# A mixture of experts and a LoRA layer in float32: one transfer of 256 KB per sample instead of four of 64 KB

## What is computed

```python
w = weight[adapter_ids]
y = jnp.einsum('bsi,boi->bso', x, w)
...
h = jnp.einsum('bsd,nrd->nbsr', y, lora_A)
coef = (SCALE * lora_weights)[:, None, None]
lora_out = jnp.einsum('nbsr,nor->bso', h, lora_B * coef)
out = x + jnp.einsum('bsd,od->bso', y, W) + bias + lora_out
```

## Time and profile before

| | |
|---|---|
| profiled execution | 1567.71 us |
| its span | 1566.0 us |
| median of three runs | 1570.32 us |
| PE busy | 1499.9 us (96%) |
| DVE, ACT, POOL busy | 780.1, 387.2, 470.0 us |
| stage one | products from 36 to 819 us |
| stage two | from 841 us to the end |
| moved by DMA | 257.74 MB, mean 165 GB/s |
| transfers of line 179 | 576 of 64 KB, median 3.0 us from issue to landing |

### The profile page before, as it was taken

One profiled execution on the slowest core, in us unless ns is written; L12 is line 12 of the kernel. 1 busy time (PEld: TensorE's weight loads), 2 busy tenths in 40 slices (PEclk: granted clock), 3 DMA queues, 4 the chain that ended last, 5 costly groups with the idle time before them and its releaser, 6 DMA issues.

```text
span 1566.0 us, 28094 instructions
## 1 busy us (share of the span) xinstructions
PE 1499.9 (96%) x6356; PEld 1198.7 (77%) x6357; DVE 780.1 (50%) x1202; ACT 387.2 (25%) x493; POOL 470.0 (30%) x656
## 2 busy tenths in 40 slices
PE   5849999999999999999996999999999999999998
PEld 3738888888888888888874888888888888888886
DVE  6556566766667666377764433333333333333331
ACT  4233333433433333244433110101010101010100
POOL 3433542334433433623332222222222222222221
PEclk9979999999999999999997999999999999999999
DMA  8987678858788776688867655555555555555553
GB/s 230 234 192 162 177 181 186 199 144 198 180 195 198 191 174 158 175 189 191 192 150 202 164 139 147 134 147 134 147 134 147 134 147 134 147 134 147 134 134 80
DMA packets 174549, 257.74 MB, mean 165 GB/s; under 512 B 22720, under 2 KB 130240, under 8 KB 174528
## 3 DMA queue, kind: packets, MB, share of 16 engines
q1 hardware_dynamic: 102944, 138.97, 38.4%
q10 hardware_dynamic: 52000, 76.57, 19.6%
q0 software_dynamic: 19584, 41.98, 9.7%
HBM read 181.93 MB, written 79.69 MB: 167 GB/s over the span
## 4 chain that ended last, share of the span: by engine, by line
PE 82%; DMA 6%; DVE 4%; issue 4%; ACT 2%; ACTq 1%; DVEq 1%; SPq 1%; POOLq 0%; POOL 0%
PE ps L632 27%; PE ps L633 27%; PE ps L634 27%; DMA w_raw<-in_L_cond_weight_dram 3%; DVE w_turn L437 1%; DVE w_lo L507 1%; DMA x_raw<-in_x_dram 1%; DVE x_turn L527 1%; ACT w_hi L333 1%; DMA w_raw<-weff 1%; DMA coef<-_L_ffn_lora_weights_dram 1%; SPq L192 1%; DMA weff<-stage 0%; ACT x_hi L341 0%; POOL x_raw L179 0%
## 5 line engine op out<-in xcount | busy, mean ns | idle before, releaser
L632 PE MATMUL ps<-w_hi,x_hi 128*128 x2096 | 832.8, 397 | 32.0 <-ACT stage L358 21.7
L633 PE MATMUL ps<-w_lo,x_hi 128*128 x2096 | 831.8, 397 | 0.0
L634 PE MATMUL ps<-w_hi,x_lo 128*128 x2096 | 831.5, 397 | 0.0
L632 PEld LDWEIGHTS ps<-w_hi,x_hi 128*128 128x128 f32 x2096 | 395.7, 189 | 130.0 <-issue 34.4
L634 PEld LDWEIGHTS ps<-w_hi,x_lo 128*128 128x128 f32 x2096 | 395.6, 189 | 96.1
L633 PEld LDWEIGHTS ps<-w_lo,x_hi 128*128 128x128 f32 x2096 | 395.8, 189 | 95.6
L179 POOL DMA_DIRECT2D x_raw<-in_x_dram x576 | 308.5, 540 | 508.1 <-DVE x_turn L527 364.2
L341 ACT ACTIVATE x_hi<-x_turn 128x512 fp32r<-128x512 f32 x272 | 160.2, 626 | 762.7 <-DVE x_turn L527 439.2
L313 POOL TENSOR_TENSOR stage<-stage,w_raw 128x1024 f32<-128x1024 f32 x64 | 154.0, 2407 | 566.1 <-DMA stage<-in_x_dram 566.1
L527 DVE STREAM_TRANSPOSE x_turn<-x_raw 128x256 f32<-128x256 f32 x544 | 193.7, 415 | 162.4 <-DMA x_raw<-in_x_dram 113.4
L534 DVE TENSOR_TENSOR x_lo<-x_turn,x_hi 128x512 fp32r<-128x512 f32 x272 | 177.4, 689 | 167.0 <-ACT x_hi L341 165.7
(11 more groups left out here) (75 smaller groups left out, 26.5 us busy)
## 6 DMA issues: line engine op xcount, KB each, us to landing
w_raw<-in_L_cond_weight_dram SPq DMA_DIRECT2D x256, 256.0 KB, 5.8
x_raw<-in_x_dram POOLq DMA_DIRECT2D x576, 64.0 KB, 3.0
y_scr<-stage ACTq DMA_DIRECT2D x144, 256.0 KB, 3.9
x_raw<-y_scr SPq DMA_DIRECT2D x128, 256.0 KB, 2.7
stage<-in_x_dram SPq DMA_DIRECT2D x128, 256.0 KB, 3.7
out_dram<-stage ACTq DMA_DIRECT2D x128, 256.0 KB, 2.9
weff<-stage ACTq DMA_DIRECT2D x8, 512.0 KB, 6.9
weff<-in_L_ffn_W_dram POOLq DMA_DIRECT2D x8, 512.0 KB, 14.9
```

Source lines behind the costliest of these rows:

```text
L632: mm(ps[b][:, cols], x_hi[b][:, t, :], hi, start=t == 0, stop=False)
L633: mm(ps[b][:, cols], x_hi[b][:, t, :], lo, start=False, stop=False)
L634: last = mm(ps[b][:, cols], x_lo[b][:, t, :], hi, start=False, stop=t == KT - 1)
```

## The change

`load_sample` issues one transfer of 256 KB onto all 128 partitions in place of the four. Its source is the sample, walked as segment q, then token pair j, then token m of the pair, in pieces of 256 numbers (1 KB), as before. DVE waits for one count of 16 on the sample's semaphore instead of four.

```diff
--- before.py
+++ after.py
@@ -174,10 +174,8 @@
             if not (isinstance(n, int) and n < 2):
 
                 eng.wait_ge(x_turned, 2 * n - 2)
-            rows = x[bass.ds(sample, 1)].rearrange("a (j m) n -> (a j) m n", m=2)
-            for q in range(QUADS):
-                eng.dma_start(x_raw[b][BLK * q:BLK * (q + 1), 2 * h:2 * h + 2, :],
-                              rows[:, :, q * SEG:(q + 1) * SEG]).then_inc(x_loaded[h][b], 16)
+            rows = x[bass.ds(sample, 1)].rearrange("a (j m) (q n) -> a q j m n", m=2, q=QUADS)
+            eng.dma_start(x_raw[b][:, 2 * h:2 * h + 2, :], rows).then_inc(x_loaded[h][b], 16)
 
         @block.sync
         def _(sp):
@@ -514,7 +512,7 @@
                         split_w(k, par, c - 1)
                 split_w(k, par, chunks[-1])
 
-            def prepare_x(n, b, raw, load, loaded=x_loaded, loads=QUADS):
+            def prepare_x(n, b, raw, load, loaded=x_loaded, loads=1):
 
                 for sems in loaded:
                     dve.wait_ge(sems[raw], load * (16 * loads) + 16 * loads)
```

## The result

The forecast was 1560.7 us, faster. The changed kernel is **slower**: its median is 1582.49 us (four runs, 1581.69 to 1583.7) beside 1570.17 us for the kernel before, 12.3 us more, a ratio of 1.0082 with a 95% interval of 1.0065 to 1.0098. The profiled execution took 1582.76 us with a span of 1581.1, against 1566.0 before. The interval leaves no doubt that it is slower, by under 1%. `load_sample`'s transfer is now line 178; all later lines stand two earlier than before.

A forecast was written before the change was run, and what follows sets the result against it. PE was 96% busy; GpSimd's issue of x bounded its second gap, expert 1's weights the first. Gains of 7.6 + 2.0 = 9.6 us took 1567.71 to 1558.1; 2.6 for the median made 1560.7 us, range 1556 to 1571.

The forecast's parts named there:

- Step 2: Landing of x: a new transfer lands 2.6 us after the end of its issue, bounds 2 and 6 us.
- The rival: Loads of x: 4 segments outermost in the source put each sample on 4 DMA engines; 1566.6 us, chance 0.30.
- the 2.0 are gone: First gap of PE: with each sample on 4 engines, tile 4 costs 2.4 us, cancelling the forecast's gain of 2.0.
- Step 4: First gap of PE, ending at 100.78 us: the first fold starts 2.4 us earlier, 2.0 us gained.
- tiles 0 to 2: nothing, 1 us either way: Start of the kernel, x landing among weights and stores: no gain counted, 1 us either way kept for the range.
- Step 5: Between 101 and 819 us: earlier x gains nothing; delayed weights could cost, with slot 66's margin at 2.2 us.
- Step 3: Gap of PE at unused slots 67 to 71: PE resumes at 833.0 instead of 840.65, 7.6 us gained.
- Step 1: GpSimd's issue of x: 1.50 us a sample instead of 2.36, bounds 0.86 and 2.16.
- The dearer issue: GpSimd's issue of x: a source order unlike the target's costs, say, 5 us a sample; 1588 us, chance 0.06.
- the same four engines every time: Stage one: x always on four engines, 2.5 us or more lost per slot; over 1700 us, chance 0.04.
- Step 6: Second stage: takes its activations from SP and keeps its time.
- the signs named in the prediction: Right: about 12672 packets, first fold at 54 us; wrong: landing over 5 us, PE gap near slot 66 or 41.

The follow-up runs named there:

- tail_one: Kernel before, with one transfer per sample (4 segments outermost in the source) for tiles 68 to 71 alone; 1566.55 us, ratio 0.9984.
- wide_all: Changed kernel with 128 steps outermost in the source instead of 4 (pieces of x permuted, layer not computed); 1562.72 us, ratio 0.9958 to the kernel before.
- eight_all: Changed kernel with 8 steps outermost in the source instead of 4 (pieces of x permuted, layer not computed); 1562.05 us, ratio 0.9953 to the kernel before.
- tail_wide: Kernel before, with one transfer per sample, 128 steps outermost in the source, for tiles 68 to 71 alone; 1562.92 us, ratio 0.9957.
- four_narrow: Kernel before with its four transfers per sample, each with 4 steps outermost in the source (layer not computed); 1613.12 us, ratio 1.0278.
- mid_late: Kernel before, with POOL reading the table three more times before the second sample of each of tiles 6 to 67; 1617.57 us, ratio 1.0302.

## Why the prediction was wrong

**Step 2, the landing, failed, and it failed first.** It took 2.6 us from the end of issue, the value of the small transfers; measured were 7.9 - 1.33 = 6.6 us in the middle and 7.8 from the start of the issue at the tail. The small transfers' row was one for an even spread, and the step carried it over to a transfer whose spread was not known. The rival named exactly this spread, for a reason in the code, and got 0.30 where the forecast got 0.48, because no row showed such a transfer. The even spread was as little shown for a source with 4 outermost, so "no row shows it" should have weighed on both alike. (The chances themselves are slightly off: slower has 0.12, but the two slower rivals have 0.10.)

**The rival's own size was wrong too.** It had the spread, and gave 1566.6 us. It priced the last four tiles (5.1 us) about right: the gap shrank by 4.5 us, and tail_one won 3.0. Its other terms were "the 2.0 are gone" at the start, where 7 to 8 us went (10.4 in the profiled execution), and "0 to 2" for the middle, where 8.5 went. These two turned the sign.

**Step 4 and "tiles 0 to 2: nothing, 1 us either way".** The step looked at the backlog behind the fold (54 to 86 us), found the engines 0.30 busy there, and counted on starting the fold 2.4 us earlier. What decided lay before it, from 20 to 50 us, where the engines were 0.96 busy before the change and nobody could be delayed for nothing. With 65 GB/s less in that stretch, ACT's last store of the fold went out 8.95 us later, and the fold started 6.1 us late, not 2.4 us early. With the even spread it did start early, at 52.29 in wide_all, 4.2 us before 56.50. PE resumed at 99.73, only 1.05 us earlier, which is within the 98.8 to 102.5 us of kernels that start as before. So no run shows the 2.0 us of this step, and an earlier fold did not bring them.

**Step 5, the middle, failed on the margin.** The step put nothing down, on the condition that the spread stays even, and read its margin of 2.2 us from the x of slot 66 in a kernel in which x was on time. In the changed kernel DVE is late again and again. Counted from PE's resumption, it starts to turn tile 20 at 169.9 us instead of 164.1, tile 50 at 498.1 instead of 498.2, tile 62 at 642.5 instead of 636.6, and tile 66 at 708.4 instead of 701.6. So it falls up to 7 us behind and catches up in between, and in the last slots the 2.2 us are gone. The condition, "with the same bytes over the same engines it holds", was right as a condition; wide_all and eight_all met it or came near it, and lost nothing there.

**Step 3, the second gap, was about right for an even spread.** PE was to resume 14.0 us after the last used slot; in wide_all it did so after 14.6, in tail_wide after 14.9, behind ACT, as written. That wide_all's 832.92 meets the 833.0 is partly luck: its last used slot ended at 818.37 and not at 819.08. With the narrow spread the gap is bound by landings.

**Step 1, the issue,** was 1.50 us with bounds of 0.86 and 2.16; it measured 1.33. The dearer issue (chance 0.06) is out. So are the same four engines every time: PE kept its 0.233 us a product from 111 to 779 us but for 1.0 us. Which engines carry which sample the profile doesn't name. The Trainium skill (same page and section) says that GpSimd's transfers take their k engines in turn; the trace agrees as far as that PE stayed at full pace. **Step 6** held within 0.6 us.

Of the signs named in the prediction, the packets, a landing over 5 us, the fold's start and a wait of PE at slot 66 (824.20) all showed it wrong.

## What to carry to other kernels

When small transfers are merged, look at the outermost dimension of the merged source and target, not only at bytes and counts: here 4 outermost made the merged transfer land after 7.8 us and cost 12.3 us, while the kernels with 8 and 128 outermost (which mix up the pieces of x) were 7 us faster than before. The queue's packets, divided by its transfers, showed the spread: 272, 144 and 80 for 4, 8 and 16 engines. Try such a change one part of the program at a time: the last four tiles were worth 3.0 us alone, 6.6 with an even spread, and that was hidden behind two parts that lost.

## What the runs showed of the hardware that was not expected

- The time that GpSimd takes to issue a transfer depends on its spread: 256 KB in 256 pieces of 1 KB took 0.72 us over 16 engines, 0.93 over 8 and 1.33 over 4; 64 KB in 64 pieces took 0.53 and 0.74. Pieces alone don't explain it; the number of packets, 80, 144 and 272, rises with it (0.21 us for 64 more, 0.40 for the next 128).
- An uneven spread brings packets of its own, under 512 B: with 4 engines, 272 packets for 64 of data. The DMA share in the middle rose from 0.79 to 0.84 at the same GB/s. These packets alone are not what cost the start: four_narrow has just as many of 16 bytes, 192 a sample, moved 257 GB/s from 20 to 50 us instead of 214, and its first gap ended at 99.39. What is left is that an engine gets 64 KB at once; that this is the cause is argued and not shown. In the middle no run separates the two.
- A short wait of PE costs more than itself. The one of 3.95 us at 824.20 was followed by 5 us at a granted clock of 0.50, and its slot took 2.6 us longer. In mid_late, nine waits of 32.3 us came with a loss of 47.6 us.
